# Post-norm decoder layer: softmax sums from ScalarE's accumulator, four heads' values side by side

## What is computed

```
x = layernorm(x + attention(x))     # 16 heads of 32 channels, causal, Wq Wk Wv Wo with biases
x = layernorm(x + wkv(k=x, v=ctx))  # a running weighted mean along the tokens, per channel
x = layernorm(x + mixture(x))       # 16 query heads; one key head and one value head, picked
                                    # per token by a gate; causal softmax again
softmax(scores)[q, k] = exp(s[q,k] - max_k s) / sum_k exp(s[q,k] - max_k s)
```

## Time and profile before

| what | value |
|---|---|
| median of 3 runs | 1739.58 us (1738.91 to 1740.75) |
| the profiled execution | 1745.21 us, span 1743.3 us |
| mean granted TensorE clock | 0.952 of full speed |
| busy share of the span: PE, DVE, ACT, POOL | 84%, 63%, 37%, 23% |

### The profile page before, as it was taken

One profiled execution on the slowest core, in us unless ns is written; L12 is line 12 of the kernel. 1 busy time (PEld: TensorE's weight loads), 2 busy tenths in 40 slices (PEclk: granted clock), 3 DMA queues, 4 the chain that ended last, 5 costly groups with the idle time before them and its releaser, 6 DMA issues.

```text
span 1743.3 us, 29718 instructions
## 1 busy us (share of the span) xinstructions
PE 1459.9 (84%) x9792; PEld 1147.2 (66%) x9792; DVE 1106.6 (63%) x2267; ACT 646.1 (37%) x1456; POOL 396.3 (23%) x541
## 2 busy tenths in 40 slices
PE   4667989889898988989898898988898898989655
PEld 4546767767666767766677676666677676667443
DVE  3346585766758576675857566685856667585644
ACT  2224252533425343342524344252424334253312
POOL 1013140221414032230413123041312304140210
PEclk8678999999999999999999999999999999999778
DMA  5223232231323222132323213132321313232010
GB/s 140 76 76 82 66 83 71 50 88 37 93 56 82 70 65 72 46 85 55 91 67 70 67 41 92 46 91 67 74 67 51 96 34 97 55 85 56 13 49 13
DMA packets 63282, 118.24 MB, mean 68 GB/s; under 512 B 14480, under 2 KB 32912, under 8 KB 63248
## 3 DMA queue, kind: packets, MB, share of 16 engines
q1 hardware_dynamic: 63248, 117.80, 26.7%
HBM read 32.81 MB, written 8.39 MB: 24 GB/s over the span
## 4 chain that ended last, share of the span: by engine, by line
PE 52%; DVE 25%; issue 8%; ACT 7%; DMA 3%; POOL 1%; SPq 1%; DVEq 1%; ACTq 0%; POOLq 0%
PE pp L411 11%; PE pp L413 10%; PE pp L412 10%; PE po L509 5%; DVE neg_max L1150 4%; PE sq L457 2%; DVE w_max L1220 2%; DVE w_key L1225 2%; PE po L513 2%; DMA q_stack<-max_rows 2%; DVE w_val L1316 2%; PE po L523 2%; DVE o_tok L1175 2%; ACT prob L870 2%; DVE stats L1181 1%
## 5 line engine op out<-in xcount | busy, mean ns | idle before, releaser
L870 ACT ACTIVATE prob<-sk 128x512 f32<-128x512 f32 x384 | 215.1, 594 | 428.7 <-PE sk L436 427.4
L1150 DVE TENSOR_REDUCE neg_max<-sq 128x2 f32<-128x512 f32 (+1 forms) x384 | 249.7, 678 | 48.5 <-PE sq L436 40.5
L411 PE MATMUL pp<-xt_hi,w_hi 128*128 128x256 f32 x768 | 233.3, 304 | 32.4 <-DVE w_lo L1137 14.5
L412 PE MATMUL pp<-xt_lo,w_hi 128*128 128x256 f32 x768 | 220.2, 287 | 0.0
L413 PE MATMUL pp<-xt_hi,w_lo 128*128 128x256 f32 x768 | 220.0, 286 | 0.0
L411 PE MATMUL pp<-w_hi,xt_hi 128*128 128x512 f32 x384 | 170.5, 444 | 26.5 <-DVE w_val L1316 22.2
L411 PEld LDWEIGHTS pp<-xt_hi,w_hi 128*128 128x128 f32 x768 | 150.0, 195 | 41.6 <-issue 26.1
L412 PE MATMUL pp<-w_lo,xt_hi 128*128 128x512 f32 x384 | 159.4, 415 | 0.0
L413 PE MATMUL pp<-w_hi,xt_lo 128*128 128x512 f32 x384 | 159.1, 414 | 0.0
L412 PEld LDWEIGHTS pp<-xt_lo,w_hi 128*128 128x128 f32 x768 | 150.2, 196 | 0.7
L413 PEld LDWEIGHTS pp<-xt_hi,w_lo 128*128 128x128 f32 x768 | 150.0, 195 | 0.0
(11 more groups left out here) (158 smaller groups left out, 3267.1 us busy)
## 6 DMA issues: line engine op xcount, KB each, us to landing
q_stack<-q_hi SPq DMA_DIRECT2D x256, 128.0 KB, 2.3
q_stack<-q_lo SPq DMA_DIRECT2D x128, 128.0 KB, 2.3
k_stack<-k_hi SPq DMA_DIRECT2D x128, 128.0 KB, 2.3
x_raw<-in_xT SPq DMA_DIRECT2D x16, 512.0 KB, 3.5
k_stack<-k_lo SPq DMA_DIRECT2D x64, 128.0 KB, 2.3
xa<-in_x SPq DMA_DIRECT2D x16, 512.0 KB, 3.3
w_val<-in_ctxT SPq DMA_DIRECT2D x64, 128.0 KB, 2.1
out_y<-xb SPq DMA_DIRECT2D x16, 512.0 KB, 2.8
```

What stands on the lines that cost most here:

```text
L411: T.matmul(out, lh, rh, start=(c == 0), stop=False, skip_group_check=True)
L412: T.matmul(out, lh, rl, start=False, stop=False, skip_group_check=True)
L870: A.activation(dst, sk[n % 2][:], ACT.Exp, scale=SCALE).then_inc(s_exp, 1)
L1150: V.tensor_reduce(dst, src, AX.X, ALU.max, negate=True).then_inc(s_max, 1)
```

## The change

The sums are no longer a column of the value product. After `maxima`, ACT makes the exponential of the query-major scores in place, head by head with the head's maximum as bias, and lets its accumulator give the row's sum (`totals`). The scale moves into Wq and its bias. A bank `sq` is now free after `totals`, not after `maxima`. DVE inverts the sums from SBUF (`inverse`). With no 33rd column, the values of four heads lie side by side in 32 columns of the array each, and the product fills half a bank. In the first attention the result stays channel-major: `repeat_a` makes PE repeat the inverted sums over the 32 channels of each head, ACT copies them (`copy_r`), and DVE multiplies (`normalise_a`); `turn_a` and `out_transpose` are gone. The third block still turns its result, with two transposes. All five orders are written anew.

```diff
-            def scores_sq(b, g, tiles, stk, per, key, s_sq, s_max):
+            def scores_sq(b, g, tiles, stk, per, key, s_sq, s_sum, s_last, last):
...
                     if n >= 2:
-                        pe.wait_ge(s_max, TILES * b + n - 1)
+                        pe.wait_ge(s_sum, TILES * b + n - 1)
+                    elif s_last is not None:
+                        pe.wait_ge(s_last, last - 1 + n)
...
+            def values(b, g, value, s_exp):
                 pe.wait_ge(s_exp, TILES * b + 3 * (g + 1))
+                for k in range(HG):
+                    T.matmul(po[HD * k:HD * (k + 1), 0:S], value(0, HG * g + k), prob0[:, k, :],
+                             start=True, stop=False, skip_group_check=True)
+                for k in range(HG):
+                    mm = T.matmul(po[HD * k:HD * (k + 1), P:S], value(1, HG * g + k), prob1[:, k, :],
+                                  start=False, stop=True, skip_group_check=True)
+            def turn_f(b, g):
+                pe.wait_ge(f_och, NG * b + g + 1)
                 for c in range(TT):
+                    mm = T.transpose(po[:, S + P * c:S + P * (c + 1)], o_ch[:, P * c:P * (c + 1)], ident[:])
...
+            def repeat_a(b, g):
...
+                pe.wait_ge(a_rec, NG * b + g + 1)
+                for c in range(TT):
+                    for k in range(HG):
+                        mm = T.matmul(po[HD * k:HD * (k + 1), S + P * c:S + P * (c + 1)],
+                                      o_rec[:, g % 2, c, k:k + 1].to_broadcast([P, HD]), ident[:],
+                                      start=True, stop=True, skip_group_check=True)
...
-                    A.activation(dst, sk[n % 2][:], ACT.Exp, scale=SCALE).then_inc(s_exp, 1)
+                    A.activation(dst, sk[n % 2][:], ACT.Exp).then_inc(s_exp, 1)
...
+            def totals(b, g, tiles, s_max, s_sum):
+                for i in tiles:
+                    n = 3 * g + i
+                    act.wait_ge(s_max, TILES * b + n + 1)
+                    c, heads = (0, range(HG)) if i == 0 else (1, range(2 * (i - 1), 2 * i))
+                    keys = P * (c + 1)
+                    for k, h in enumerate(heads):
+                        score = sq[n % 2][:, keys * k:keys * (k + 1)]
+                        e = A.activation(score, score, ACT.Exp, bias=neg_max[:, g % 2, h, c:c + 1],
+                                         accum_out=row_sum[:, g % 2, c, h:h + 1])
+                    e.then_inc(s_sum, 1)
...
+            def copy_r(b, g):
+                act.wait_ge(a_rt, NG * b + g + 1)
+                A.activation(w_d[:, HC - 1, :], po[:, S:2 * S], ACT.Copy).then_inc(a_rch, 1)
...
+            def inverse(b, g, s_sum, s_rec):
+                dve.wait_ge(s_sum, TILES * b + 3 * (g + 1))
+                V.reciprocal(o_rec[:, g % 2], row_sum[:, g % 2]).then_inc(s_rec, 1)
...
+            def normalise_a(b, g):
+                dve.wait_ge(a_pv, NG * b + g + 1)
+                wait(dve, ot_hi, NG * b + g)
+                V.tensor_tensor(o_tok[:].rearrange("p c d -> p (c d)"), po[:, 0:S], w_d[:, HC - 1, :], ALU.mult)\
+                    .then_inc(a_norm, 1)
```

More of the change, by code:

```diff
@@ L498, in scores_sk @@
                     mm.then_inc(s_sk, 1)
-            def values(b, g, value, s_exp, s_norm, s_pv):
-                if g:
-                    pe.wait_ge(s_norm, NG * b + g)
+            def values(b, g, value, s_exp):
                 pe.wait_ge(s_exp, TILES * b + 3 * (g + 1))
[L505 to L512, removed]
-                        mm = T.matmul(po[VW * j:VW * j + HD + 1, at + P:at + S], value(1, HG * g + k), prob1[:, k, :],
-                                      start=False, stop=True, skip_group_check=True)
-                mm.then_inc(s_pv, 1)
@@ L517, in turn @@
-            def turn(b, g, s_och, s_po):
-                pe.wait_ge(s_och, NG * b + g + 1)
-                for c in range(TT):
-                    for pair in range(HG // 2):
-                        at = P * (HG // 2 * c + pair)
-                        mm = T.transpose(po[:, at:at + P], o_ch[:, pair, P * c:P * (c + 1)], ident[:])
-                mm.then_inc(s_po, 1)
-            def out_transpose(b, g, s_before, before):
-                pe.wait_ge(a_norm, NG * b + g + 1)
-                wait(pe, s_before, before)
-                for c in range(TT):
-                    mm = T.transpose(pt[:, P * c:P * (c + 1)], o_tok[:, c, :], ident[:])
-                mm.then_inc(a_job, 1)
+                for k in range(HG):
+                    T.matmul(po[HD * k:HD * (k + 1), 0:S], value(0, HG * g + k), prob0[:, k, :],
+                             start=True, stop=False, skip_group_check=True)
@@ new lines, in max_f @@
+            def max_f(b, g):
+                max_transpose(f_max, TILES * b + 3 * (g + 1), f_free, F_JOBS * b + F_M[g], f_job, g)
+            def repeat_a(b, g):
+                if g:
+                    pe.wait_ge(a_norm, NG * b + g)
+                else:
+                    if not (isinstance(b, int) and b < 2):
+                        pe.wait_ge(f_norm, NG * (b - 1))
+                    wait(pe, a_norm, NG * b)
+                pe.wait_ge(a_rec, NG * b + g + 1)
[4 more added lines that the diff above has]
+                                      start=True, stop=True, skip_group_check=True)
+                mm.then_inc(a_rt, 1)
@@ L993, in iteration @@
                     exps_a(t, 1, 2)
+                    copy_r(t, 1)
+                    totals_a(t, 2, 0, 1)
                 if prev:
@@ L1354, in iteration @@
                 if do_a:
-                    normalise_a(cha, t, 0)
+                    maxima_a(t, 1, 2)
+                    normalise_a(t, 0)
+                    rows_a(t, 1)
                     if not prev:
```

467 lines of the change are left out of this document (235 added, 232 removed).

## The result

The changed kernel takes 2133.6 us (median of 4, 2128.2 to 2137.6) beside 1740.2 of the kernel before (4 runs): ratio 1.224, interval 1.220 to 1.228. I forecast 1940, range 1730 to 2005. Slower was right, the size was wrong by 194 us, as much again as the loss that I had forecast (200).

A forecast was written before the change was run, and what follows sets the result against it. PE led at 84% busy, waiting for DVE in part of the iteration. Eight walked stretches gave +15.4 us, 13.3 taken; over fifteen iterations +200 us on 1745.2 gives 1945, so 1940 us, range 1730 to 2005.

The forecast's parts named there:

- a1-a2: Stretch from the first `sk` of first attention's group 1 to group 2's: 12.7 us, was 11.0.
- f3-a0: Stretch from third block's group 3 to first attention's next group 0: bound by DVE, 15.4 us, was 12.3.
- predicted walk: Eight stretches between groups' first `sk`, followed through PE, ACT and DVE: sum 115.1 us against 99.7, +15.4.
- the sum at the old clock: Whole kernel: 13.3 us more in each of fifteen steady iterations, +200 us on 1745.2, giving 1945, so 1940.
- Rival (4): PE's gaps lower the clock to 0.90: some 40 us of products on the path take 4 more; 2000 us, chance 0.06.
- I take 13.3 of it: Of the eight stretches' +15.4 us an iteration only 13.3 counted, since overlaps are unseen and some link will be shorter.
- PE's edits: PE's work an iteration: values -5.8 us, turns -4.0, `repeat_a` 2.2 more; net about -7.4.
- Rival (3): Four heads on PE don't run beside each other: values 1.42 us, repeat 1.0; 1.7 an iteration, 1965 us, chance 0.08.
- The path: From the start of `row_hi` to a group's first `sk`: 2.9 us.
- `sk` <- DMA: Sign: scores waiting for the maxima rows are PE's largest wait, 15 to 25 us an iteration.
- Rival (1): PE's work decides: 7.4 us go, idle time grows by 3 only; -4.4 an iteration, 1674 us, chance 0.16.
- Rival (2): Only PE's missing cover counts, DVE's and ACT's orders don't: +4.0 us an iteration, 1800 us, chance 0.20.

The follow-up runs named there:

- e7_warm_all: Changed kernel with 74 useless products an iteration in PE's long waits, in numbers after the length of the waits: 2043 us.
- e10_all_k0: e9 with SP issuing next group 0's `k_stack` ahead of the third block's last maxima rows, and no useless products ahead of first query-major scores: 1911 us.
- e5: Changed kernel with `row_hi` and `copy_f` ahead of tile 2's sums (2056 us), plus first `out_hi` behind group 1's exponentials: 2043 us.
- e9: Changed kernel with e5's moves, first attention's group 0 rows earlier on ACT and DVE, and the useless products of e7_warm_all: 1937 us.
- e8: Changed kernel without the sums (one exponential of one column per tile, no accumulator read), with 72 useless products an iteration in PE's waits: 1900 us.
- e13: Changed kernel with the four moves of e10_all_k0 (`row_hi` and `copy_f`, `out_hi`, group 0's rows, `k_stack`) and no useless products: 1977 us.
- e11: Kernel before with the transposes of five groups' maxima in the middle of the projection that follows instead of ahead of it: 1785 us, +42 us.
- e12: Kernel before with ACT repeating the copy of first attention's group 0 maxima rows eight times (some 2.8 us) in 13 iterations: +28 us.

## Why the prediction was wrong

```
                 a1-a2 a2-a3 a3-f0 f0-f1 f1-f2 f2-f3 f3-a0 a0-a1   sum
before            11.0  16.7  13.2   8.5  15.1  12.5  12.7  10.5  100.2
predicted walk    12.7  16.9  17.6  12.2  13.3  15.6  15.4  11.4  115.1
after             15.5  18.7  17.5  12.9  15.1  15.0  18.4  12.9  126.0
e7_warm_all       16.4  17.2  17.5  12.3  12.8  15.3  17.0  10.8  119.4
e10_all_k0        13.7  17.2  16.9  11.6  12.1  14.9  13.7  10.7  110.8
after, low        9.5   3.4   0.0   1.6   5.0   3.1  10.2   9.1   41.9
```

- *The step that failed is the sum at the old clock.* The walk reckoned every chain at the durations of the kernel before, a clock of 0.99, and the sum has no term for the clock. Rival (4) had it as an alternative with 0.06, at 0.90 and +4 us. It was 0.83. (The row behind it, is the stretch from 95 to 197 us, not the first 102 us.) With the useless products the walk is met within 0.6 us in six of eight stretches (all but a1-a2 and f3-a0). Of the 10.9 us by which it was short, at least 6.6 are clock (126.0 - 119.4). PE is idle for 27 of 126 us, and the granted clock is 0.83. The Trainium skill (TensorE: Matmul & The Clock Gate, A second HAM failure mode: psum-queue depth-cycling) describes such a case in another kernel, whose engine pauses often and briefly between groups of matmuls and swings between the two levels; the trace agrees that it swings, and doesn't show what makes it. I had cited the rule on gaps and then held the rival's price to 4 us: I took 40 us of products on the path and a tenth of clock, where a third of the iteration ran at half the clock.
- *Two DMA waits were missed.* `out_hi(t, 0)` waits for the last `k_stack` transfer and now stands ahead of the exponentials of group 1. Moving it gave 13 us at the low clock (e5); what it costs at the upper level no run shows by itself. `sq` of the next sequence waits 1.68 us for the `k_stack` of group 0, which SP issues behind the third block's last rows (1.6 us in f3-a0, e10 against e9 at the upper level).
- *What is left of the 10.9 us* behind the 6.6 lies, by e7, in a1-a2 (3.7 above the walk) and f3-a0 (1.6), less 1.0 in the other six. The wait for `k_stack` has the size of the 1.6. In a1-a2 e7 still has 6.8 us at the lower level, which cost 2.9 in e8's pair. So the clock's part would be some 9.5 of 10.9; this is an estimate and no proof, for e8 has no sums and the costs act on each other: e10's four moves without useless products (e13) take 156 us off, of which the clock gives back a part (41.9 to 20.9 us low).
- *"I take 13.3 of it"* was wrong in direction: with most of the clock back, in e7, six of eight stretches are as long as walked and two longer. With 15.4 the forecast would have been some 30 us better, and still 160 short.
- *PE's edits*: values 958.72 - 957.93 = 0.79 us a group, predicted 0.7, was 1.42; `repeat_a` 0.57 (956.74 - 956.17 in the same timeline), predicted 0.55. Rival (3) is dead. The Trainium skill (TensorEngine Tiling (Array Packing), Theoretical Speedup) has up to four times the speed for at most 32 columns and up to two for at most 64; the trace has 1.8 times from the one to the other.
- *`totals`*: pairs start every 0.34 us at 128 and 0.45 at 256 columns in the timeline, predicted 0.39 and 0.49. ACT's iteration has 63.7 us of work, predicted 66; its share is 49%, not 58, mainly since the iteration grew.
- *The path*: the chain from `row_hi` (914.30) to `sk` (917.15) is 2.85 us, predicted 2.9. `sk` <- DMA is PE's largest wait, 162.6 + 131.4 = 294 us, 18 an iteration, as forecast (15 to 25).
- *Rival (1)*, faster, fell: PE's idle time grew by 15.5, not 3. *Rival (2)*, cover only (+4.0 an iteration): e11 measured 3.0 for five of the eight groups on the kernel before, some clock included. It is real, and a part of the whole.
- What stays open: which share of the clock's cost is on the path (over 90 us; the useless products can't say how much over), and what in the pattern of gaps keeps PE at the lower level at 78% busy while the kernel before, 88% busy, stays at the upper.

## What to carry to other kernels

An edit that takes work off the leading engine can slow that very engine: when the walk over the stretches says that its idle time doubles, give the clock a term in the sum and not only a rival. Its price can be read where one trace passes the same iteration at both levels (2.9 us for 6.8 at the lower level in e8, 1.6 for 3.4 in e9, 0.8 for 6.6 in e12's a0-a1: it depends on what else the stretch waits for). Where a step is put ahead of another on an in-order engine, list every semaphore that it waits for, its DMAs too. To price the clock apart from the chains, fill the waits with useless products: what the time falls by is a lower bound of its cost. Before the difference of two runs is put down to one edit, compare the time at the lower level in the same stretch: e9 against e7 looked like 2.7 us for one moved line, and is in large part clock.

## What the runs showed of the hardware

The lower level held for 23.9 us in which PE was busy for 18.7, and a kernel got faster by 90 us (4.2%) with 74 useless products added to each iteration. Two passes of the same stretch in one execution took 16.6 us with 6.8 at the lower level and 13.6 without. In the kernel before, a wait longer by some 2.4 us in each iteration left the clock of the middle at 0.98, with the lower level behind it in about every second iteration. Four column groups of 32 made the values 1.8 times as fast as two of 33 columns.
